# Four graph layers on one core: the last tile of each GENConv pass summed piece by piece, three table loads and a weight load at other places, two activations in another order

## The reference

```python
msg = relu(x[src]) + 1e-7
w = segment_softmax(msg * t, dst)
aggr = segment_sum(msg * w, dst)
h = (x + aggr) @ W1                      # 128 -> 256
h = (h - mean(h)) * rsqrt(var(h) + 1e-5) * gamma + beta
x = relu(relu(h) @ W2)                   # 256 -> 128
```

## Time and profile before

| | us |
|---|---|
| median of 3 runs | 2814.39 |
| lowest, highest run | 2811.42, 2818.41 |
| the profiled execution | 2816.33 |
| its span, first to last instruction | 2814.6 |
| TensorE busy, all products | 2355.3 |
| VectorE busy | 1685.2 |
| ScalarE busy | 774.2 |
| GpSimd busy | 1362.1 |

### The profile page before, as it was taken

The page is one execution under the profiler, slowest core; times in us unless marked ns, Lnnn a source line. Parts: engine busy times, 40 slices in busy tenths (PEclk is TensorE's granted clock), DMA queues, the critical chain, the costliest instruction groups (busy, mean ns, idle before and its releaser), DMA issues. The chain is left out here.

```text
span 2814.6 us, 47730 instructions
## 1 busy us (share of the span) xinstructions
PE 2355.3 (84%) x9448; PEld 1517.2 (54%) x9449; DVE 1685.2 (60%) x5131; ACT 774.2 (28%) x1807; POOL 1362.1 (48%) x1336
## 2 busy tenths in 40 slices
PE   3577768877889998987988798879975999999997
PEld 1233345546788888864544354435434555555554
DVE  7999931114777677744267426732674676666665
ACT  1233301112122222211111311121112555555553
POOL 2200000001777777734783477257750776666660
PEclk9999978887555555568999899999997555555556
DMA  0000010001444444421110011011113222222220
GB/s 9 3 0 0 0 37 0 0 0 57 118 119 117 116 119 118 117 76 34 17 17 10 10 17 17 9 11 17 17 13 122 64 61 59 58 58 58 58 59 27
DMA packets 197073, 128.29 MB, mean 46 GB/s; under 512 B 138144, under 2 KB 179993, under 8 KB 195872
## 3 DMA queue, kind: packets, MB, share of 16 engines
q0 software_dynamic: 40256, 60.21, 10.0%
q1 hardware_dynamic: 151820, 59.71, 8.7%
q10 hardware_dynamic: 4822, 6.56, 0.7%
HBM read 106.83 MB, written 13.34 MB: 43 GB/s over the span
## 5 line engine op out<-in xcount | busy, mean ns | idle before, releaser
L1704 PE MATMUL ps<-adj,small 125*128 (+1 forms) x3150 | 631.3, 357 | 0.0
L1429 POOL DMA_INDIRECT edge_rows<-pay,small x425 | 513.9, 1209 | 129.2 <-issue 128.0
L1887 POOL DMA_INDIRECT adj<-h_rows,adj x416 | 396.3, 953 | 180.2 <-issue 101.7
L1704 PEld LDWEIGHTS ps<-adj,small 125*128 125x128 bf16 x3150 | 311.1, 99 | 275.3 <-issue 12.6
L1114 POOL DMA_INDIRECT work<-p_rows,small x416 | 395.2, 950 | 128.5 <-issue 111.1
L1281 PE MATMUL ps<-work 128*128 x1024 | 297.9, 445 | 20.5 <-DVE work L1172 18.5
L2059 PEld LDWEIGHTS ps<-adj 128*128 128x128 f32 x928 | 214.8, 321 | 173.1 <-issue 112.6
L2059 PE MATMUL ps<-adj 128*128 128x125 f32 x928 | 280.7, 456 | 21.6 <-DVE work L1962 21.1
L2049 PE MATMUL ps<-adj 48*128 48x256 f32 x464 | 282.9, 712 | 0.5 <-ACT adj L1997 0.4
L1292 PE MATMUL ps<-small,work 128*128 128x64 f32 x1024 | 250.5, 399 | 38.7 <-issue 37.6
L1292 PEld LDWEIGHTS ps<-small,work 128*128 128x128 f32 x1024 | 239.1, 322 | 57.0 <-issue 55.5
(11 more groups left out here) (339 smaller groups left out, 2873.9 us busy)
## 6 DMA issues: line engine op xcount, KB each, us to landing
work<-dst_all SPq DMA_DIRECT2D x256, 64.0 KB
work<-edge_attr SPq DMA_DIRECT2D x256, 64.0 KB
edge_rows<-pay,small POOLq DMA_INDIRECT x425, 2.7
work<-p_rows,small POOLq DMA_INDIRECT x416
adj<-h_rows,adj POOLq DMA_INDIRECT x416
adj<-adj SPq DMA_DIRECT2D x232, 24.0 KB
pay<-edge_pay SPq DMA_DIRECT2D x106, 46.9 KB
work<-x_kept SPq DMA_DIRECT2D x2, 1562.5 KB, 6.4
```

The lines of the kernel that those rows point to most:

```text
L1429: eng.indirect_dma_start(edge_rows[:, :], bass.IndirectOffsetOnAxis(ap=place[:, k:k + 1], axis=0), pay[:, k * ROW:(k + 1) * ROW], None).th ...
L1704: ins = eng.matmul(ps[:, j, 0:cw], parts[k][:, i * D:(i + 1) * D], cols, start=first and i == 0, stop=last and i == 2, skip_group_check=True)
L1887: eng.indirect_dma_start(gathered[:, at:at + D], None, h_rows[:, :], bass.IndirectOffsetOnAxis(ap=row3_i[:, c, DST_C:DST_C + 1], axis=0)). ...
```

## The change

Six edits.

1. In the last tile of either pass the products stand piece by piece: piece 0 with the three parts, then piece 1, and so on.
2. The wait ahead of the W2 load is for the first piece of `s_h`, not for the seventh.
3. The table set of the exponential is loaded at the top of a layer, ahead of the wait for `s_fin`; that of the root right after the tile loop, ahead of the wait for `s_h`.
4. The layernorm loads the root's set at its start.
5. Of the 14 scalings, pieces 0 and 1 of `k` = 0 are made before the root of `k` = 1; the remaining 12 after it, piece by piece.
6. TensorE's wait for them counts accordingly: 3 for piece 0, 4 for piece 1, then 2j + 2 as before.

```diff
@@ layernorm, scalar
             if fetch:
                 fetch_rows(G, fetch, eng, 1, s_fetch)
+            eng.preload_act_table_set("sqrt_and_others")
             for j, c0, cw in PIECES:
                 eng.wait_ge(s_d, j + 1)
@@ genconv, scalar
+            def relu(k, j, c0, cw):
+                eng.activation(h1[k][:, c0:c0 + cw], h1[k][:, c0:c0 + cw], ACT.Relu,
+                               bias=shift[:, k:k + 1], scale=scale[:, k:k + 1]).then_inc(s_r1, 1)
+
             with eng.Fori(0, AL) as l:
-
+                eng.preload_act_table_set("exp_and_others")
                 eng.wait_ge(s_fin, l + 1)
...
-                eng.wait_ge(s_h, (l + 1) * NP)
+                eng.preload_act_table_set("sqrt_and_others")
+                eng.wait_ge(s_h, l * NP + 1)
                 eng.dma_start(w2, a["agg_w2"][:, bass.ds(l * 2, 2), :]).then_inc(s_w2, 16)
                 for k in range(2):
                     for j, c0, cw in PIECES:
                         eng.wait_ge(s_h1, l * (2 * NP) + k * NP + j + 1)
                         eng.activation(h1[k][:, c0:c0 + cw], ps[:, j, 0:cw], ACT.Copy).then_inc(s_h1o, 1)
+                    if k == 1:
+                        eng.wait_ge(s_aff, l * 2 + 1)
+                        for piece in PIECES[0:2]:
+                            relu(0, *piece)
                     eng.wait_ge(s_var, l * 2 + k + 1)
                     eng.activation(sd, mv[:, 1:2], ACT.Sqrt, bias=epsc).then_inc(s_sd, 1)
+                eng.wait_ge(s_aff, l * 2 + 2)
                 for j, c0, cw in PIECES:
-                    for k in range(2):
-                        if j == 0:
-                            eng.wait_ge(s_aff, l * 2 + k + 1)
-                        eng.activation(h1[k][:, c0:c0 + cw], h1[k][:, c0:c0 + cw], ACT.Relu,
-                                       bias=shift[:, k:k + 1], scale=scale[:, k:k + 1]).then_inc(s_r1, 1)
+                    if j >= 2:
+                        relu(0, j, c0, cw)
+                    relu(1, j, c0, cw)
@@ genconv, tensor
-                            for i in range(3):
-                                for j, c0, cw in PIECES:
...
+                            each = [(i, *piece) for i in range(3) for piece in PIECES]
+                            if last:
+                                each = [(i, *piece) for piece in PIECES for i in range(3)]
+                            for i, j, c0, cw in each:
...
                 for j, c0, cw in PIECES:
-                    eng.wait_ge(s_r1, l * (2 * NP) + 2 * j + 2)
+                    eng.wait_ge(s_r1, l * (2 * NP) + max(2 * j + 2, 4 if j == 1 else 3))
                     eng.matmul(ps[:, j, 0:cw], w2[:, 0, :], h1[0][:, c0:c0 + cw], start=True, stop=False)
```

32 lines of the change are left out of this document (16 added, 16 removed).

## The result

The changed kernel takes 2803.76 us (median of seven runs, 2800.63 to 2805.74); the kernel before took 2818.41 us in seven runs beside it (2811.42 to 2820.80). The ratio is 0.9953, with a 95% interval of 0.994 to 0.9965: 13 us less by the ratio (10 to 17 by its interval), 14.65 between the two medians. The profiled execution's span went from 2814.6 to 2798.9 us.

The account below looks back on a forecast made before the run. TensorE was taken to bound GENConv's first pass, VectorE the second, waits between engines the turns. Terms 5.7 + 1.9 + 3.85 + 1.28 + 1.3 = 14.0 us off 2816.33, less 1.94, gave 2800.4 us; range 2795 to 2806.

Parts of the forecast that it names:

- Wait for the first sum: After GENConv's second pass: VectorE's 6.1 us wait over three layers shrinks to 0.12 a layer; gain 5.7 us, bounds 5.4 and 6.1.
- First pass, together with the exponential's load: VectorE's copies after the first pass end sooner, 1.9 us; exponential's table load moves into ScalarE's idle time, 3.85 us.
- Root's table and the scalings ahead of the second root: Small network: early root load gives 0.2 us, two moved scalings give it back; sum 0, bounds -0.6 and +0.6 over three layers.
- take 2 x 0.66 us ... end near 1556.45: Two moved activations start 1.32 us before the second root and fill ScalarE's idle, so the root gets back 0.2 us late.
- Twelve scalings instead of thirteen at the end: After the second root ScalarE turns 0.66 us earlier to the last outputs where TensorE isn't last; 1.3 us, bounds 0 and 2.0.
- In layer 1 it is: Layer's end: in layer 1 TensorE is last, starting at the low clock after 3.90 us idle, so the gain doesn't count.
- Layer 3 looks like layer 2: Layer's end: as in layer 2, the clock stays high and TensorE isn't last, so two layers gain 0.66 us each.
- Layernorm's table: Last layernorm: load moved into ScalarE's 6.47 us idle gains 1.28 us; the other three get a covered load.
- The products of a piece hinder each other: Last tiles: three products into one bank wait for each other, 2.2 us a last tile; 2807.0 us in all; chance 5%.
- A table switch costs more than its load: ScalarE must empty itself before each switch; four switches give 5.6 us more gain, 2794.8 us; chance 4%.
- The early loads do not do what they say: Tables are loaded again at first use, so 5.1 us of gain fall away: 2805.5 us; chance 4%.
- The loops run worse: Two tile passes: new instructions make each of 66 loop turns stand 0.43 us longer, 28 us: 2829 us; chance 3%.

Follow-up runs that it names:

- the edit alone: Kernel before with only the last tile's 21 products of either pass ordered piece by piece: 3385.12 us against 3392.28, ratio 0.9976.
- the two written out: Changed kernel with 25 tiles a pass written out, 2773.59 us; the same with ScalarE's three last outputs among its scalings, 2771.22 us.
- the changed kernel's second execution: Changed kernel again, unchanged, on the chip with slower scatters: 3390.19 us against 3407.12 for the kernel before, ratio 0.9957.
- The kernels with one part alone: Kernel before with one part each: order by pieces, ratio 0.9976; three early table loads, 1.0005; two moved scalings, 1.0002; second weights' earlier load, 0.9999.

## Why the prediction was right, point by point

The predicted time was 2800.4 us, the measured one 2803.76, inside the range. The predicted gain of 14.0 us stands against 14.65 between the two medians and 15.7 between the two spans. The 3.4 us by which the time is off lie in the start: the prediction took 2814.39, the median of three runs, and over seven runs the same kernel has 2818.41. The parts:

- **Wait for the first sum: predicted 5.7, measured 5.6** (6.1 to 0.5 us), by the edit alone as well. The 0.12 us put in for a dependent step was 0.18.
- **First pass, together with the exponential's load: predicted 5.7, measured 4.6 to 5.4** by the stage table, and 6.0 at the places. From the start of the last tile to the last copy it is 5.44 us in all six layers of the kernel before, and 4.77 in all nine of the changed kernel and the two written out on this kind of chip: 0.67 a layer against 0.62. The load is gone from its old place, the step from the exponents to the exponential is 1.27 us shorter, and the one to TensorE's first product 4.0 us over three layers. What the table has less lies in the tiles between, where the kernel before differs by 0.8 us from itself.
- **Root's table and the scalings ahead of the second root: predicted +0.2 and -0.2 a layer, measured +0.19 and -0.06.** The first half was right. The step that failed is "take 2 x 0.66 us ... end near 1556.45": it gave the root all of the 0.2 us back late. The pair takes 1.40 us, yet the root starts 1.31 us after the pair's start, 0.11 us after its variance. A net gain of 0.13 us a layer, inside the bounds of 0.6.
- **Twelve scalings instead of thirteen at the end: predicted 1.3, measured 1.9 to 2.2** between the first profiles. The mechanism was right. What was wrong was to tie the clock to the layer ("In layer 1 it is", "Layer 3 looks like layer 2"): which layers have TensorE at 1.2 GHz from the first product on changes from execution to execution of one kernel, with the moment at which the clock rose in the stage before (as shown with the changed kernel's second execution). In such a layer the edit gives next to nothing (*end* is 15.45 to 15.75 us with thirteen scalings and 15.51 to 15.62 with twelve); elsewhere 0.65 us. So it is 0 to 2 us over three layers, as the bounds had it.
- **Layernorm's table: predicted 1.28, measured 1.28 at the place; 0.7 from the first centred piece to the end.** The time from the sums to the root fell from 1.38 to 0.10 us. From the root to the end it is 8.71 us in the profile before and 9.40 after; over all profiles these lie at 8.69 to 9.89 without the early load and at 8.84 to 9.57 with it. So it is spread and no answer to the edit, as the two ranges overlap; that TensorE's clock makes it was not separated. The three other layernorms' squares are not late (0.03 us after the first centred piece, as before), but they got a load that they did not need. One thing was foreseen nowhere: in the second layernorm the root starts 0.40 us after the sums in all eight kernels with the early load and 0.10 in all five without. The load itself is over 3.25 us before the squares; what takes these 0.3 us no run shows.
- **Second weights: predicted 0, measured 0.** 7.514 us and 7.516 us, once the time at the low clock is taken out.
- **Unasked: 0.2 to 1.6 us in the second pass and 0.8 to 1.5 us *to variance 1*.** The kernel before differs by 1.4 and 0.7 us in these stages from itself, so no edit is to be credited; in *to variance 1* the difference is the clock alone.
- **The sums.** Two of them don't come out. The chance of "faster" is given as 0.86, but the parts named (0.78, 0.04, 0.04 and half of 0.06) make 0.89, which leaves 0.08 and not 0.11 for "same". And the upper bounds of the gain add up to 15.8 us, so to 2797.6 with the microsecond for the clock; the range goes on to 2795 without a term for it. Neither decides whether the measured time falls into the range.

The rivals. *The products of a piece hinder each other*: refuted, 4.13 to 4.17 us for 21 products by pieces, and the 42 at a pass's end take 8.16 us and not 8.18. *A table switch costs more than its load*: refuted, two loads leave a gap of 2.60 us and cost 2.71. As for the rule cited in the prediction (the Trainium skill, ScalarE: Activation LUTs, section "What ACT_TABLE_LOAD costs"), its 1283 ns of load is what the rows show and its drain of 1380 ns is in none of them, with ScalarE idle or busy ahead of the load. *The early loads do not do what they say*: refuted, no load stands at the exponential or the root. *The loops run worse*: refuted for this change; the loop body's own cost is real, though, and was the larger prize: 12 us a layer, that no part of the change touched.

Measured at their places, the edits explain a gain of 5.6 (wait) + 2.0 (copies) + 4.0 (exponential) + 0.4 (root and scalings before it) + 0 to 2 (end) + 1.3 - 0.3 (layernorms) = 13.0 to 15.0 us. The kernels with one part alone show the terms for the wait, the exponential, the root, the end and the last layernorm by their rows, not by their totals: on that chip only the first total differs, and the four together come to 2 us less where the changed kernel has 17. The copies were not taken alone on a chip where their stage is quiet; that term rests on the changed kernels' rows.

The total came as near as it did partly by luck: 2.2 us at the end in place of 1.3 came from the clock, which was high at the start of all three products in this execution, and in another execution of the same kernel it was high in one.

## What to carry to other kernels

When two engines take turns on one buffer, order the producer's last round so that the first piece is finished first: here it turned 2.04 us of waiting a layer into 0.18 at no cost for TensorE, where VectorE needs 1.26 us for a piece that comes every 0.59. Between the passes, where a copy takes as long as a piece, VectorE still waits between copies and the gain is 0.67 us. Load activation tables where ScalarE waits for something else; each was worth its 1.28 us, and only where it stood on the path. And before trimming the turns of a loop, compare the loop's period with its engines' own work: here VectorE's 0.65 us a tile over TensorE's pace were worth 27 us in the stages and 30 between the medians, twice what all six edits gave.

## What the runs showed of the hardware

**One kernel, two kinds of chips.** The kernel before takes 2818 us on one and 3392 or 3407 us on the other. Whether a chip keeps to its kind no run shows. Two executions of the changed kernel are 591 us apart. Up to the first layernorm's table load, 652 us into the program, they are the same. From there to the second one's lie 219 us of it (GpSimd gathers rows, L1115), to the third one's 197 (GENConv, with the scatters) and to the fourth one's 175 (gathers again, L1898); behind that nothing. The scatters themselves keep their pace: a layer's first 136 take 204 to 206 us in all 13 profiles. But in the first 205 us of them TensorE makes 630 products with `adj` on the slower kind and 942 on the faster. From the changed kernel on the slower kind, ScalarE's first operation of some tiles of the first pass, and GpSimd's last scatter of that layer:

```profile
1609.28 0.28 ACT L1631 ACTIVATE small<-ps 125x128 bf16<-125x128 f32 x1 [6.88 <-remote]
1616.86 0.28 ACT L1631 ACTIVATE small<-ps 125x128 bf16<-125x128 f32 x1 [7.02 <-remote]
...
1725.64 1.19 POOL L1430 DMA_INDIRECT edge_rows<-pay,small  x1 [0.30 <-issue]
...
1737.33 0.28 ACT L1631 ACTIVATE small<-ps 125x128 bf16<-125x128 f32 x1 [3.52 <-PE ps L1694]
1741.49 0.28 ACT L1631 ACTIVATE small<-ps 125x128 bf16<-125x128 f32 x1 [3.61 <-PE ps L1694]
```

This tile takes 7.58 us while scatters run (from the sixth tile on they take 5.2 to 8.2 us, and 6.2 on average over the pass), and one after the last of them 4.16 us. The same kernel on the faster kind, with scatters running:

```profile
1585.85 0.28 ACT L1631 ACTIVATE small<-ps 125x128 bf16<-125x128 f32 x1 [3.58 <-PE ps L1694]
1589.95 0.28 ACT L1631 ACTIVATE small<-ps 125x128 bf16<-125x128 f32 x1 [3.56 <-PE ps L1694]
```

4.10 us a tile. That the excess goes with GpSimd's indirect DMAs is shown by where it begins and ends; why the engines slow down with them on one chip and not on the other stays open. Leaving the scatters out wasn't tried, because the next phase reads the rows that they write.

**The clock after a short idle.** After 3.77 us of idle ahead of the same products, in the same kernel, TensorE starts at the low clock in two layers of one execution (1.84 us for the pair) and at the high one in the third and in all layers of another execution (0.99 to 1.09 us). After 3.90 us in the kernel before it is one layer of three, in one execution the first and in the other the second. So the length of the idle time alone does not tell; the stage before does (10.42 us or more of *to variance 1* in every layer that starts low, 10.37 or less in every other).

**A long loop body has a price at its back branch**: VectorE stands 3.44 and 3.41 us there instead of 0.82, against 12 us gained in each second pass.
